# One cross-attention stage on one core: pieces of the next unit's row maxima at other places in the step, the closing and turning transposes beside the value products, GpSimd adding eleven and ten tiles in turn

## The reference, cut to what matters

```python
q = _qdq(x) @ _qdq(wq).T + bq            # 16 heads of 32 features
kv = cond @ wkv.T + bkv
attn = softmax(einsum("bnhd,bmhd->bhnm", q, k) / sqrt(32))
o = einsum("bhnm,bmhd->bnhd", attn, v)
```

## Time and profile before

| | |
|---|---|
| three runs | 2582.46, 2584.22, 2582.68 us; median 2582.68 |
| the profiled execution | 2584.68 us, its span 2582.9 us |
| TensorE busy | 2515.3 us, 97% of the span |
| VectorE / ScalarE / GpSimd busy | 1788.7 (69%) / 1233.5 (48%) / 1287.2 us (50%) |
| the first attention's steps | from about 630 to 1400 us of the span |
| of it, 920 to 968 us (48 us) | PE 46.66, DVE 34.26, ACT 29.59, POOL 45.96 us busy, granted clock 1.00 |

### The profile page before, as it was taken

How to read it: one execution, slowest core, us unless ns; L and a number is a source line. 1 busy time by engine, 2 the same in 40 slices (tenths; PEclk the granted TensorE clock), 3 DMA queues, 4 the chain that set the end, 5 groups by cost and what they waited for, 6 DMA issues and landing times. The chain is left out here.

```text
span 2582.9 us, 33907 instructions
## 1 busy us (share of the span) xinstructions
PE 2515.3 (97%) x13273; PEld 1624.9 (63%) x13288; DVE 1788.7 (69%) x2455; ACT 1233.5 (48%) x1853; POOL 1287.2 (50%) x340
## 2 busy tenths in 40 slices
PE   8999999999999999999998999999999999999998
PEld 8988888987544545545544787888533333334786
DVE  4554554556767767767774676674799999999873
ACT  3221312311666666666664232322588888886110
POOL 0000000000999999999994000000499999997310
PEclk9999999999999999999999999999999999999999
DMA  8677776655535345345313753542997777776400
GB/s 301 215 249 241 263 277 240 220 180 156 107 80 119 72 87 112 72 93 109 68 66 114 261 183 135 181 155 79 251 213 165 167 160 167 157 173 192 126 33 33
DMA packets 218864, 405.10 MB, mean 157 GB/s; under 512 B 18216, under 2 KB 94536, under 8 KB 218640
## 3 DMA queue, kind: packets, MB, share of 16 engines
q1 hardware_dynamic: 218704, 402.93, 56.4%
HBM read 260.63 MB, written 140.59 MB: 155 GB/s over the span
## 5 line engine op out<-in xcount | busy, mean ns | idle before, releaser
L1458 POOL TENSOR_TENSOR pooled<-pooled,probs 128x2048 f32<-128x2048 f32 x140 | 641.1, 4579 | 21.0 <-POOL pooled L1458 0.9
L1305 ACT ACTIVATE probs<-psum 128x512 f32<-128x512 f32 (+1 forms) x832 | 458.7, 598 | 338.8 <-PE psum L1196 334.2
L1332 DVE TENSOR_REDUCE win_max<-psum 128x1 f32<-128x802 f32 x480 | 455.4, 988 | 151.4 <-PE psum L1161 151.0
L2236 DVE TENSOR_SCALAR probs<-psum,bound 128x1024 f32<-128x1024 f32 (+1 forms) x416 | 498.9, 1274 | 31.3 <-POOL pooled L2268 19.5
L2211 ACT ACTIVATE probs<-probs 128x1024 f32<-128x1024 f32 (+1 forms) x416 | 437.6, 1059 | 82.2 <-DVE probs L2236 40.6
L2268 POOL TENSOR_TENSOR pooled<-pooled,probs 128x2048 f32<-128x2048 f32 x92 | 424.2, 4610 | 12.8 <-ACT probs L2211 0.2
L1196 PE MATMUL psum<-q_st,k_st 128*128 128x512 f32 (+1 forms) x832 | 334.6, 439 | 18.5 <-ACT probs L1305 12.1
L296 POOL TENSOR_TENSOR r_q<-ve_q,minus_half 128x4 f32<-128x4 f32 x8 | 9.1, 1132 | 611.3 <-DVE ve_q L256 611.3
L1196 PEld LDWEIGHTS psum<-q_st,k_st 128*128 128x128 f32 (+1 forms) x832 | 149.1, 185 | 240.8 <-ACT probs L1305 179.2
L1161 PE MATMUL psum<-k_st,q_st 96*128 96x402 f32 x960 | 266.7, 359 | 6.1 <-DVE o_sb L1363 5.1
L2179 PE MATMUL psum<-q_st,k_st 128*128 128x512 f32 (+1 forms) x832 | 250.7, 426 | 12.9 <-DVE probs L2236 9.8
(11 more groups left out here) (271 smaller groups left out, 4281.8 us busy)
## 6 DMA issues: line engine op xcount, KB each, us to landing
k_st<-k_hi SPq DMA_DIRECT2D x64, 801.0 KB, 9.2
k_st<-k_lo SPq DMA_DIRECT2D x48, 801.0 KB, 11.0
k_hi<-kt_hi SPq DMA_DIRECT2D x32, 801.0 KB, 3.6
k_lo<-kt_lo SPq DMA_DIRECT2D x32, 801.0 KB, 5.8
v_rows<-v_out SPq DMA_DIRECT2D x96, 256.0 KB
v_st<-v_rows SPq DMA_DIRECT2D x24, 768.0 KB
q_st<-q_hi SPq DMA_DIRECT2D x64, 256.0 KB, 7.9
w<-w_hi_d SPq DMA_DIRECT2D x64, 256.0 KB, 3.1
```

The lines of the kernel that those rows point to most:

```text
L1305: A.activation(probs[i % NPROBS][0:rows, j, :], bank(score_banks.where["score", u, t, j])[0:rows, :], ACT.Exp, scale=1.0 / ROOT).then_inc( ...
L1332: V.tensor_reduce(win_max[:, r, j, c:c + 1], window(windows.where["max", u, i])[:, :, 0:MV], AX.XY, ALU.max).then_inc(max_done, 1)
L1458: G.tensor_tensor(pooled[u % 2][:], before[:], probs[tile(u, k) % NPROBS][:], ALU.add).then_inc(pool_added, 1)
L2236: V.tensor_scalar(probs[i % NPROBS][0:rows, half * W:half * W + W, :], window(("score", u, t, half))[0:rows], bound[0:rows, u // NG, t:t + 1],
```

## The change

Four edits, all in `attention_0`. The number of pieces, scores and value products stays. (1) On TensorE the second piece of a step moves from before the value products to between s2 and s3, and the third from before s3 to behind it. (2) `closing` and `turn` move from the step's end to directly behind the value products, ahead of s2; on VectorE the closing moves ahead of the step's second piece. (3) The sums are turned by four plain products with four columns of the identity as the moving side, in place of four transposes of 128 columns; VectorE reads their result from 16 columns side by side. (4) Units with an odd number give GpSimd ten tiles, those with an even number eleven as before, the last still seven; the tile that is no longer pooled is summed on TensorE.

```diff
 def pooled_tiles(u):
-    return 11 if u < UNITS - 1 else 7
+    return 11 - u % 2 if u < UNITS - 1 else 7
...
 # closing, on TensorE
-for w, src in enumerate((acc_sb, den_sb)):
-    for r in range(RT):
-        m = M.transpose(window(slot)[:, w, r * P:(r + 1) * P], src[:, r * P:(r + 1) * P],
-                        ident[:])
+for r in range(RT):
+    M.transpose(window(slot)[:, 0, r * P:(r + 1) * P], acc_sb[:, r * P:(r + 1) * P], ident[:])
+for r in range(RT):
+    m = M.matmul(window(slot)[:, 1, r * HPG:(r + 1) * HPG], den_sb[:, r * P:(r + 1) * P],
+                 ident[:, 0:P:DH], start=True, stop=True)
...
 # the step, on TensorE
-if coming[1:]:
-    max_of(*coming[1])
 if behind:
     values(*behind)
...
 if now:
-    scores(*now, 2)
-if coming[2:]:
-    max_of(*coming[2])
-if now:
-    scores(*now, 3)
     if now[1] == CLOSE_AT and now[0]:
         closing(now[0] - 1)
     if now[1] == TURN_AT and now[0] + 1 < UNITS:
         turn(now[0] + 1)
+    scores(*now, 2)
+if coming[1:]:
+    max_of(*coming[1])
+if now:
+    scores(*now, 3)
+if coming[2:]:
+    max_of(*coming[2])
...
 # the step, on VectorE
-if now and now[0] + 1 < UNITS:
-    for i in windows_at(now[1]):
-        max_of(now[0] + 1, i)
+coming = [(now[0] + 1, i) for i in windows_at(now[1])] if now and now[0] + 1 < UNITS else []
+for one in coming[:1]:
+    max_of(*one)
 if now and now[1] == CLOSE_AT and now[0]:
     closing(now[0] - 1)
+for one in coming[1:]:
+    max_of(*one)
```

More of the change, by code:

```diff
@@ L1358, in closing @@
                         V.wait_ge(closed_ps, u + 1)
-                        s = own.after(V.reciprocal(rec[:], ps[:, 1, 0:S:DH].rearrange("p (r j) -> p r j", j=HPG)))
+                        s = own.after(V.reciprocal(rec[:], ps[:, 1, 0:RT * HPG].rearrange("p (r j) -> p r j", j=HPG)))
                         if u:
```

## The result

The changed kernel takes 2627.48 us (median of 4 runs, 2626.99 to 2628.85) against 2583.45 before (2582.46 to 2584.52). The ratio of the times is 1.0171, 95% interval 1.0158 to 1.0183: 44 us slower. The forecast was 2628 and slower.

A forecast was written before the change was run, and what follows sets the result against it. TensorE's row was taken to set the pace, through waits for VectorE's reductions. Units 1 to 14 add 36.3 us, unit 0 2.1, the last closings 1.3, the tiles 6.2: together 45.9, so 2628 us, range 2602 to 2641.

The forecast's parts named there:

- The ordinary step: TensorE, between value products: 3.75 us with the moved pieces, +0.24 in five three-bank steps, +0.17 in four two-bank steps a unit.
- The unit's end: TensorE, steps 10 to 12: turning loses its cover, +0.44; step 12 loses a piece, -0.36; step 10 0; together +0.08 us.
- The closing step: TensorE, the step that holds the closing: from 4.76 to 5.39 us, +0.63; with cheap sums -0.07.
- x: TensorE time of the four plain products for the sums in a closing: taken as 0.80 us, lower end 0.1.
- The two last closings: Closings in unit 15 and after it, counted at 0.63 us each, together 1.3.
- Ten tiles: Seven odd units: one tile's sums move from GpSimd to TensorE, 0.89 us each, 6.2 us in all.
- GpSimd as no bound: First attention: GpSimd already idles 0.75 us a unit and its result lies ready 5 us, so its relief is worth nothing.
- Rival (a): TensorE's ordinary steps: the clump of pieces is broken up and runs without waits, 3.24 us a step; 2560 us, chance 0.07.
- Rival (b): First attention: GpSimd sets the pace, seven additions less save 33 us; 2550 us, chance 0.03.
- rival (c): Ordinary steps: waits only change place, steps stay at 3.51 to 3.58 us; 2600 us, chance 0.11.
- The sum: Whole kernel: all terms together, 45.9 us slower, which gave 2628 us.
- A full unit: Each of units 1 to 14: 1.20 + 0.68 + 0.08 + 0.63 = 2.59 us slower, 36.3 in all.

The follow-up runs named there:

- Experiment 1: Kernel before with only the second and third pieces of the maxima moved to their new places on TensorE: 2606.0 us against 2583.4, ratio 1.0086.
- Experiment 6: Changed kernel with VectorE reducing only 200 of the 401 columns of each bank: 2566.6 us, ratio to the kernel before 0.9938.
- Experiment 2: Kernel before with only closing and turning moved directly behind the value products, on VectorE the closing ahead of the third piece: 2590.2 us, ratio 1.0026.
- experiment 4: Kernel before with only GpSimd's tiles changed, ten instead of eleven in units 1, 3, ..., 13: 2590.8 us, ratio 1.0026.
- Experiments 7 to 9: Kernel before with halved reductions (2572.0 us); with pieces spread in steps 5 to 10 (2572.1); spread plus ten GpSimd tiles every second (2568.6) or third unit (2567.3).
- Experiment 8: Kernel before with pieces spread in steps 5 to 10, value products between the first and second piece: 2572.1 us, ratio 0.9960.
- experiment 9: Kernel before with pieces spread in steps 5 to 10 and ten GpSimd tiles in every second unit (2568.6 us, 0.9944) or every third (2567.3 us, 0.9934).
- experiment 3: Kernel before with only the sums' four transposes replaced by four plain products with four moving columns: 2588.75 us, ratio 1.0018.

## Why the prediction was right, point by point

**The ordinary step** (+0.24 five times, +0.17 four times a unit). Right, in mechanism and size. The changed kernel shows 3.75 with three score banks and with two (992.06 to 995.81), and with sums 4.62 (987.44 to 992.06) where 4.46 stood; 1.62 from m1 to m0', 0.47 and 0.33 behind it. Experiment 1 measures the places alone at +22.6 us, where the prediction's terms give 15 x (1.20 + 0.68 - 0.36) = 22.8. Experiment 6 shows the cause: take away the reduction's length, and the loss is gone. One reading was a little off, with nothing worked out from it: 0.93 for each reduction but the last is the mean of three in 2.79, while one takes 0.99 and two take 1.88, so each but the last takes 0.90.

**The unit's end** (+0.44 for step 11, -0.36 for step 12, 0 for step 10). +0.40, -0.35 and 0: step 10 takes 2.61 (974.23 to 976.84), as before. Experiment 2 gives the turning alone.

**The closing step** (+0.63). It is +0.60, with x = 0.81 against 0.80. That it came out so near is two small misses that cancel in part. The values' four transposes, now behind the value products, take 0.49 and not 0.44 (1001.43 to 1001.92). The chain behind the sums was 3.06 long and not 3.16 (1002.73 to 1005.79), since VectorE is done 0.09 earlier after the last of the small products. The two last closings were booked at 0.63 each; the one in step 4 of the last unit costs 0.9 (1405.16 to 1409.06, where 1362.05 to 1365.06 stood), as its transposes had lain under a wait for ScalarE, and the one behind the stage 0.4.

**x and the rule on weight loads.** Of the two rules of the Trainium skill's page TensorE: Matmul & The Clock Gate, the one on the weight loads (LDWEIGHTS (loading the stationary operand)), which gave an estimated 0.86, comes within 6% of the 0.81 measured; the one for small moving sides (Back-to-back issue gap), which gave some 0.2, does not describe these products, each of which has weights of its own. The same section gives that table for a matmul in isolation and says that in a stream of weight loads and matmuls both set the spacing.

**Ten tiles** (+0.89 seven times, 6.2 us). 0.99 each, and +7.4 us by experiment 4: the term was a little too small, by the wait for want of a score bank that the prediction had only in its upper bound.

**GpSimd as no bound.** Right for this change, and the margin was as thin as rows 1 showed. Experiments 7 to 9 cross it: once TensorE's row falls below 47.1 us a unit, GpSimd takes over, and the fourth edit turns from a loss into a gain.

**The rivals.** Rival (a), the clump broken up, has its deciding point where it was put: with reductions of 0.57 the changed order has no wait but the 0.10 of the weight load, and gains 61 us; it doesn't have them. Rival (b) falls by experiment 4, rival (c) by experiment 1.

**The sum** (45.9). It is 44.4 at the end of the stage. A full unit costs 2.46 without the tiles (over the twelve units between GpSimd's starts at 737.57 and 1347.29) where 2.59 was booked, 1.8 less in 14 units. Unit 0 costs 1.4 (value products at 678.17 for 676.78) instead of 2.1, since its first value products start 0.4 earlier than before (639.52 for 639.95), which the prediction did not book. The tiles cost 0.7 more. That the time itself was met to 0.5 us is partly luck: these misses cancel in part, the kernel before took 0.8 us more than the 2582.7 that the forecast started from, and 2628.6 was rounded down.

## What to carry to other kernels

Where an engine hands work to another through two buffers in turn, don't count how evenly the pieces lie; measure the distance from each piece to the next but one and hold it against the time from its start to its free buffer (1.62 us here). No piece waits when every such distance is longer, with some tenth to spare for the weight load. Experiment 8 got there by putting the longest block of other work, here the value products, between two pieces instead of beside all three. And relief for a second engine is worth nothing until the first needs less time than it: the same edit lost 7.4 us in one order of the work and gained 3.5 in another.

## What the runs showed of the hardware that was not expected

- A product whose semaphore comes just in time, with no idle time on the product itself, still costs 0.10 us more than one that is free long before: its weight load waits for the same semaphore, and doesn't run ahead (experiment 6: 0.48 to the next instruction against 0.37; experiment 9: 0.57 for two scores against 0.47).
- Plain products of fp32 with four moving columns and 128 by 128 weights take 0.81 us for eight passes (experiment 3), as eight passes with 128 moving columns do in 0.80.
